# A graph-attention and mixture-of-experts kernel on one core: two of four one-hot matrices of each batch written by VectorE, two by ScalarE

## What is computed

```python
xw = (x @ W).reshape(N, H, CPH)
e = jax.nn.leaky_relu(a_s[src] + a_d[dst], NEG)
m = jax.ops.segment_max(e, dst, num_segments=N)
p = jnp.exp(e - m[dst])
alpha = p / segment_sum(p, dst)[dst]
out = jax.ops.segment_sum(xw[src] * alpha[:, :, None], dst, num_segments=N)
```

## Time and profile before

| | us |
|---|---|
| runs shown: median of 3 (lowest, highest) | 3051.76 (3049.93, 3054.21) |
| the profiled execution: its own time | 3056.89 |
| its span, first to last instruction | 3055.1 |
| busy in the span: PE, DVE, POOL, ACT | 2055.3, 2173.8, 1897.4, 1584.4 |
| batches 10 to 49: first start of L1835 to last end of L1837 | 654.7 to 1982.3 |

### The profile page before, as it was taken

The page is one execution under the profiler, slowest core; times in us unless marked ns, Lnnn a source line. Parts: engine busy times, 40 slices in busy tenths (PEclk is TensorE's granted clock), DMA queues, the critical chain, the costliest instruction groups (busy, mean ns, idle before and its releaser), DMA issues.

```text
span 3055.1 us, 42040 instructions
## 1 busy us (share of the span) xinstructions
PE 2055.3 (67%) x11266; PEld 1941.1 (64%) x11267; DVE 2173.8 (71%) x4430; ACT 1584.4 (52%) x2550; POOL 1897.4 (62%) x1880
## 2 busy tenths in 40 slices
PE   4700000068888788888888888703448999999998
PEld 2500000058788788877888887703447999999997
DVE  7677767778798788888888888788864444444443
ACT  5424333268777777777777777624432333333332
POOL 5777777777777777777777777777771222222222
PEclk8855555579899989989898999855558999999999
DMA  9446449744444444444444444465772232222222
GB/s 351 137 142 169 162 153 191 148 124 127 137 152 127 127 160 129 127 130 159 127 127 140 149 127 127 152 207 187 249 257 44 37 38 38 38 37 37 38 37 31
DMA packets 277323, 395.44 MB, mean 129 GB/s; under 512 B 154844, under 2 KB 229793, under 8 KB 270673
## 3 DMA queue, kind: packets, MB, share of 16 engines
q1 hardware_dynamic: 200977, 244.52, 25.3%
q0 software_dynamic: 74384, 146.42, 21.6%
q10 hardware_dynamic: 1840, 3.06, 0.3%
HBM read 202.05 MB, written 191.79 MB: 129 GB/s over the span
## 4 chain that ended last, share of the span: by engine, by line
POOL 45%; PE 25%; issue 16%; DVE 7%; DMA 2%; DVEq 2%; ACT 2%; SPq 1%; POOLq 0%; ACTq 0%
POOL AR L929 43%; PE ps L1445 12%; PE ps L1451 12%; DMA tables<-AR 1%; DVE group_stats L2014 1%; ACT AR L1254 1%; DMA state<-AR 1%; POOL adstart L891 1%; POOL placed L995 1%; DVE AR L1710 1%; SPq L381 0%; SPq L607 0%; PE ps L1321 0%; DVE AR L2138 0%; DVE AR L2135 0%
## 5 line engine op out<-in xcount | busy, mean ns | idle before, releaser
L929 POOL DMA_INDIRECT AR<-tables,idx x1403 | 1339.1, 954 | 429.5 <-issue 427.3
L1350 PE MATMUL ps<-table_parts,onehot 128*128 128x408 f32 (+1 forms) x5440 | 1123.5, 372 | 324.7 <-ACT onehot L1210 174.8
L1350 PEld LDWEIGHTS ps<-table_parts,onehot 128*128 128x128 f32 x5440 | 1090.1, 210 | 358.1 <-DVE AR L1837 163.0
L1135 ACT COPY AR<-AR 128x1984 f32<-128x1984 f32 (+3 forms) x110 | 400.4, 3640 | 352.4 <-DVE AR L1757 309.6
L1004 POOL DMA_INDIRECT out<-AR,idb x105 | 184.9, 1761 | 570.4 <-issue 536.7
L1757 DVE TENSOR_TENSOR_SCAN AR<-ps,AR 128x512 f32<-128x512 f32 x404 | 454.2, 1197 | 0.0
L1445 PEld LDWEIGHTS ps<-AR 128*128 128x128 f32 x3360 | 393.4, 193 | 34.3 <-issue 29.0
L1445 PE MATMUL ps<-AR 128*128 128x128 f32 x3360 | 393.9, 276 | 29.0 <-DVE AR L2233 29.0
L1750 DVE TENSOR_TENSOR AR<-AR,ps 128x3968 f32<-128x3968 f32 (+1 forms) x51 | 355.9, 6978 | 0.0
L2233 DVE COPY AR<-AR 128x1024 f32 x210 | 151.5, 722 | 207.4 <-PE ps L1445 206.0
L1210 ACT ACTIVATE onehot<-onehot 128x1536 fp32r<-128x1536 f32 (+1 forms) x160 | 250.7, 1567 | 5.1
(11 more groups left out here) (346 smaller groups left out, 2444.9 us busy)
## 6 DMA issues: line engine op xcount, KB each, us to landing
state<-AR SPq DMA_DIRECT2D x50, 2232.0 KB
AR<-tables,idx POOLq DMA_INDIRECT x1452
AR<-in_L_ffn_W SPq DMA_DIRECT2D x16, 1024.0 KB, 9.9
AR<-placed SPq DMA_DIRECT2D x420, 32.0 KB
AR<-adstart SPq DMA_DIRECT2D x50, 248.0 KB, 4.1
adstart<-room SPq DMA_DIRECT2D x21, 496.0 KB
tables<-AR SPq DMA_DIRECT2D x49, 136.0 KB, 3.2
room<-tables SPq DMA_DIRECT2D x14, 476.0 KB, 3.8
```

The source lines that it names most:

```text
L929: pool.indirect_dma_start(out=G[s][:, j, 0:ROWT], out_offset=None, in_=table_rows, in_offset=bass.IndirectOffsetOnAxis(ap=idx[:, s, j:j + ...
L1135: return S.copy(to.rearrange("p j (h c) -> p j h c", h=HD)[:, :, :, a:z], of[:, :, 1:n + 1].rearrange("p (c h) j -> p j h c", h=HD)[:, :, ...
L1350: return T.matmul(bank[:, 0:z], mark, table_parts[:, k, v * w:v * w + z], start=(a == 0 and k == 0), stop=(a == LEV - 1 and k == PARTS - 1))
```

## The change

The constant `PEA` goes from 3 to 2, so ScalarE's marks cover columns 0 and 1 (256 elements per level), TensorE's stretches only these two columns, and the part behind the stretches, renamed `last_columns`, covers columns 2 and 3. VectorE's one comparison goes over 17 x 256 elements. Two semaphores get names in the plural. The number of instructions, of matmuls and the memory stay as they were.

```diff
-PEA = 3
+PEA = 2
...
-            def last_column(b):
-
-                pe.wait_ge(last_column_marked, b - PE0 + 1)
+            def last_columns(b):
+
+                pe.wait_ge(last_columns_marked, b - PE0 + 1)
                 for a in range(LEV):
-                    for k in range(PARTS):
-                        mm = product(column_banks[PEA], onehot[:, a, PEA * P:PEC * P], a, k)
-                mm.then_inc(last_column_used, 1)
+                    for c in range(PEA, PEC):
+                        for k in range(PARTS):
+                            mm = product(column_banks[c], onehot[:, a, c * P:(c + 1) * P], a, k)
+                mm.then_inc(last_columns_used, 1)
...
-            def mark_last_column(b):
+            def mark_last_columns(b):
 
                 n = b - PE0
                 dve.wait_ge(codes_loaded[b % 2], 16 * (n // 2 + 1))
-                V.tensor_tensor(onehot[:, :, PEA * P:PEC * P], bc(column_codes[b % 2][:, PEA * P:PEC * P].unsqueeze(1), [P, LEV, P]),
-                                bc(own_code.unsqueeze(2), [P, LEV, P]), ALU.is_equal).then_inc(last_column_marked, 1)
+                V.tensor_tensor(onehot[:, :, PEA * P:PEC * P], bc(column_codes[b % 2][:, PEA * P:PEC * P].unsqueeze(1), [P, LEV, (PEC - PEA) * P]),
+                                bc(own_code.unsqueeze(2), [P, LEV, (PEC - PEA) * P]), ALU.is_equal).then_inc(last_columns_marked, 1)
```

More of the change, by code:

```diff
@@ L301, in build @@
         columns_taken = sem("columns_taken")
-        last_column_marked = sem("last_column_marked")
-        last_column_used = sem("last_column_used")
+        last_columns_marked = sem("last_columns_marked")
+        last_columns_used = sem("last_columns_used")
         parts_ready = sem("parts_ready")
@@ L745, in _ @@
                         sp.wait_ge(levels_used, len(STRETCHES) * (PE1 - PE0))
-                        sp.wait_ge(last_column_used, PE1 - PE0)
+                        sp.wait_ge(last_columns_used, PE1 - PE0)
                         for i in range(NOWN):
@@ L972, in _ @@
             pool.wait_ge(levels_used, len(STRETCHES) * (PE1 - PE0))
-            pool.wait_ge(last_column_used, PE1 - PE0)
+            pool.wait_ge(last_columns_used, PE1 - PE0)
             for n in range(4):
@@ L1399, in _ @@
                     columns(b, i)
-                last_column(b)
+                last_columns(b)
             chain(2)
@@ L1827, in take_columns @@
                 dve.wait_ge(levels_used, len(STRETCHES) * (b - PE0 + 1))
-                dve.wait_ge(last_column_used, b - PE0 + 1)
+                dve.wait_ge(last_columns_used, b - PE0 + 1)
                 for q in range(TPL):
@@ L1862, in whole_batch @@
                     own_codes()
-                    mark_last_column(PE0)
+                    mark_last_columns(PE0)
                 if by_pe(b):
@@ L1866, in whole_batch @@
                     if by_pe(b + 1):
-                        mark_last_column(b + 1)
+                        mark_last_columns(b + 1)
                 marks(NA + b, cols(b), same[:, b * J:b * J + cols(b)], VIEW[w, HD], VIEW[next_w, HD] if b + 1 < NB else None)
```

## The result

The changed kernel takes 3222.3 us (median of 5 runs, 3220.9 to 3223.3) against 3052.3 us before (5 runs): 1.0557 times as long, 95% interval 1.0545 to 1.0569, or +170 us. The profiled execution took 3222.3 us too, with a span of 3220.5 us; the profiled one of before was 4.6 us above the median of its runs, so that between the two spans there are only 165.4 us.

What follows compares the result with a forecast made beforehand. Gathers (33.72 us a batch) bound the kernel, just above a three-engine ring of 31.70; 31.70 + 2.27 - 0.86 + 3.37 + 2.2 = 38.68 us, in all +187 us, giving 3239 us, range 3150 to 3275.

Steps and rivals of the forecast that it cites:

- What bounds the kernel before: GpSimd's gathers, 33.72 us per batch, bound the kernel only just; a loop through three engines lies 2.0 us below.
- the ring: Loop per batch: VectorE's comparison to L1748, ScalarE's stretch 2 marks, TensorE's 82 matmuls, VectorE's take; 31.70 us, forecast 38.68.
- Term 1: VectorE's comparison goes from 2176 to 4352 elements, all of it on the ring: +2.27 us per batch.
- Term 2: ScalarE's marks of stretch 2 shrink: -0.86 us per batch; its other stretches shrink at nothing on the ring.
- Term 3: TensorE has 100 instead of 82 matmuls behind ScalarE's release: 18 more, +3.37 us per batch.
- Term 4: TensorE idles about 5 us per batch, so its next run starts at a lower clock: +2.2 us, ends 0 and 2.8.
- The period: Time between VectorE's takes in batches 10 to 49: 38.68 us instead of 33.95, +184.5 us over 39 periods.
- The edges: Outside the 39 periods: +4.7 us before them in batch 9, -1.9 after them as batch 49's gather wait goes.
- The sum: Whole kernel: +187 us, profiled execution from 3056.9 to 3244 us, median 3239 us.
- Faster: Rival: matmuls behind ScalarE's release hide behind VectorE's work, the gathers' 33.72 us become the period, -9 us, 3043 us; chance 0.03.

Runs made afterwards that it cites:

- experiments 6 to 8: Changed kernel and kernel before with TensorE's last-column matmuls, VectorE's comparison, or both moved in order: 3056.2, 3055.4, 3055.8 and 3055.1 us, against 3055.7 before.
- experiment 2: Kernel before, with 18 more filler matmuls ahead of the last column's 34: 3107.3 us, 1.0168 times before.
- experiment 7: Changed kernel, with VectorE's comparison moved behind ScalarE's release (L1749) and the wait for the weights: 3055.8 us, 0.9998 times before.
- experiment 5: Changed kernel, with ScalarE's Abs pass of stretches 0 and 1 done twice: 3222.9 us, 1.0547 times before.
- Experiment 6: Changed kernel and kernel before, with the matmuls of VectorE-marked columns moved between stretches 1 and 2, ahead of the wait for ScalarE: 3056.2 and 3055.4 us.
- experiment 4: Changed kernel, with 24 filler matmuls between stretches 1 and 2, where TensorE idles: 3154.1 us, 1.0323 times before.

## Why the prediction was right

The direction, the mechanism and the size hold: 3239 forecast, 3222.3 measured, inside 3150 to 3275. By its own steps:

- *What bounds the kernel before.* Right that it was the gathers: experiments 6 to 8 shorten the ring or take work off it, and the time stays. Right that the ring was only some 2 us below: of experiment 2's 3.37 us a batch, 53 / 39 = 1.4 show in the time, and 2.0 do not.
- *Term 1, the comparison, +2.27.* Measured 4.688 - 2.421 = 2.27 us. That it costs time through its place, and not by its weight, is shown by experiment 7.
- *Term 2, ScalarE's stretch 2, -0.86.* From the end of L1749 (1247.88) to TensorE's start (1251.28) are 3.40 us, where 4.27 were before: -0.87. The rest at nothing: experiment 5, for stretches 0 and 1.
- *Term 3, 18 more matmuls behind the release, +3.37.* The runs are 36 and 100, and without the slow start the 100 take 18.61 us. Experiment 6 removes this term and others with it; experiment 2 has it alone.
- *Term 4, the slow start, +2.2.* The mechanism is right, and the size was off: 20.41 - 18.74 = 1.67 us from the 40 runs, 20.24 - 18.61 = 1.63 by the two runs of experiment 4. I had averaged only the five runs after the longest idle times of before, which gave 17.58 - 15.37 = 2.21. The same trace has 14 runs of 82 after idle times of 2.1 us and more, and they average 17.20, which would have given 1.83; nine of them took 16.75 to 16.92. The choice of rows was the mistake. Its 0.53 x 39 = 21 us are nearly all of the 22 by which the difference of the spans was put too high (187 against 165). That the forecast of the median is only 17 us off is luck: I had taken off 5 us for the slower profiled execution of before, and the changed kernel's was not slower than its median. The Trainium skill (TensorE: Matmul & The Clock Gate, "What's actually happening") puts the ramp penalty below 1% of a typical kernel span. Experiment 4 took away 68 us of 3222, 2.1%, so that here the runs decide against leaving the term out: the slow start comes in each of 40 batches.
- *The period.* Takes from 659.62 to 2149.29 us are 38.20 us apart on average, 38.68 forecast. +4.25 x 39 = +165.7 us, where 184.5 were forecast.
- *The edges.* The first take came 4.9 us later (4.7 forecast). After the last take the rest is 5.2 us shorter, and not 1.9. The wait for a gather in batch 49 (1.89 us) went as forecast, and the last store lands 10.2 instead of 12.7 us after its issue. In the kernel before it started while GpSimd's 28 later loads were under way, in the changed one the last of these is done 6 us earlier than it starts; whether that is why was not tested. The remaining 0.8 us are open.
- *The sum.* 165.7 + 4.9 - 5.2 = 165.4, the difference of the spans. The medians differ by 170 us, since the profiled execution of before was slower than its median.

One reading beside the forecast fell. I took 33.95 us between the takes as a distance from the gathers' 33.72 that could be won, in the rival "Faster" and in the expectations of experiments 6 to 8. But GpSimd had no wait in these batches of the trace of before, so nothing was to be won. The takes are the wrong marks to measure by. After its first take VectorE waited 8.08 us for the batch's gathers, after its last only 1.89 us:

```profile
670.65 0.57 DVE L1729 TENSOR_TENSOR AR<-AR,ps 128x248 f32<-128x248 f32 x1 [8.08 <-DMA AR<-tables,idx]
```

The two instructions that ended these waits, at 670.65 and 1986.07, are 39 x 33.73 us apart: the gathers' own pace. So the first take was early against the gathers, and a shorter ring only makes VectorE earlier and its waits for the gathers longer.

## What to carry to other kernels

Before work is moved from one engine to another, look where it stands in both queues: a job's cost is what it puts ahead of the release that closes a ring between engines, and who else's work moves behind a wait with it. Here the work that moved was 2.3 us more on VectorE against 3.6 us less on ScalarE per batch, and the order of one loop decided about 170 us. Where two bounds are close, costs do not add up until the slack between them is spent (86 and 53 us alone, 212 together), and gains stop where the other bound stands.

## What the runs showed of the hardware

TensorE's slow start can cost more than work that prevents it: 24 matmuls of 4.6 us, put into 5.7 us of idling, made a run of 100 matmuls 1.6 us shorter and the kernel 68 us faster. I had expected it in kind. What I had not expected is that its size does not follow the idle time before the run: in the changed kernel runs of 100 took 19.9 us after 4.3 us of idling as well as 21.4. The lengths come in an order instead. They fall from batch to batch and then start again at the top, every four to six batches, through all 40:

```profile
1364.82 21.35 PE L1350 MATMUL ps<-table_parts,onehot 128*128 128x408 f32 x100 [4.35 <-ACT onehot L1210]
...
1403.90 20.68 PE L1350 MATMUL ps<-table_parts,onehot 128*128 128x408 f32 x100 [5.70 <-ACT onehot L1210]
...
1442.33 20.30 PE L1350 MATMUL ps<-table_parts,onehot 128*128 128x408 f32 x100 [5.67 <-ACT onehot L1210]
...
1480.36 20.06 PE L1350 MATMUL ps<-table_parts,onehot 128*128 128x408 f32 x100 [5.67 <-ACT onehot L1210]
...
1518.15 19.95 PE L1350 MATMUL ps<-table_parts,onehot 128*128 128x408 f32 x100 [5.76 <-ACT onehot L1210]
...
1555.84 19.89 PE L1350 MATMUL ps<-table_parts,onehot 128*128 128x408 f32 x100 [4.28 <-ACT onehot L1210]
...
1593.47 21.36 PE L1350 MATMUL ps<-table_parts,onehot 128*128 128x408 f32 x100 [4.31 <-ACT onehot L1210]
```

The granted clock stayed at 0.50 for about 6 us in the run at 1364.82 and for just under 3 us in the one at 1555.84. No run shows what sets the order. A slow start priced from a few runs can thus miss the average of 1.67 us by much: single ones are 1.2 to 2.7 us here.
